# State space loop with MLP items closed by GpSimd: how far GpSimd's inflows may run ahead of VectorE's scans

## The reference

```python
u, z = silu(conv(x @ W_in[:, :512])), x @ W_in[:, 512:]
delta = softplus(low_rank(u) @ W_dt + b_dt)
h = h * exp(delta_t * A) + delta_t * B_t * u_t      # over the 512 rows t, 16 states n
y = sum_n(h[:, n] * C_t[n]) + u * D
out = (y * silu(z)) @ W_out
mlp = (silu(x @ gate) * (x @ up)) @ down            # gate, up, down made from spline points
```

## Time and profile before

| | us |
|---|---|
| median of 3 runs (1773.16 to 1775.78) | 1775.08 |
| the profiled execution | 1770.57 |
| its span in the profile | 1768.8 |
| first loop, first scan to last product | 752.1 to 897.2 |
| second loop | 930.3 to 1073.5 |

### The profile page before, as it was taken

One profiled execution on the slowest core, in us unless ns is written; L12 is line 12 of the kernel. 1 busy time (PEld: TensorE's weight loads), 2 busy tenths in 40 slices (PEclk: granted clock), 3 DMA queues, 4 the chain that ended last, 5 costly groups with the idle time before them and its releaser, 6 DMA issues. The chain is left out here.

```text
span 1768.8 us, 26131 instructions
## 1 busy us (share of the span) xinstructions
PE 1557.7 (88%) x8448; PEld 1216.3 (69%) x8448; DVE 1230.9 (70%) x2538; ACT 938.2 (53%) x2019; POOL 732.4 (41%) x662
## 2 busy tenths in 40 slices
PE   6998958979999898888888887889999897999899
PEld 4777658967777788544533454667888686888787
DVE  5888847657787678799979995346666534666643
ACT  5555445855665556574447443235665444656543
POOL 5999833324221333187728774112212241122222
PEclk9999989989999999999999999999999998999999
DMA  3221122111112121000000000011111111111211
GB/s 124 75 73 60 36 95 86 61 52 34 48 39 87 60 87 58 27 1 1 1 27 1 1 1 6 6 33 39 47 47 63 40 68 58 49 41 39 72 54 48
DMA packets 29565, 81.47 MB, mean 46 GB/s; under 512 B 6036, under 2 KB 10904, under 8 KB 27304
## 3 DMA queue, kind: packets, MB, share of 16 engines
q1 hardware_dynamic: 28296, 74.05, 12.9%
q0 software_dynamic: 1184, 6.37, 1.1%
HBM read 79.36 MB, written 1.05 MB: 45 GB/s over the span
## 5 line engine op out<-in xcount | busy, mean ns | idle before, releaser
L880 POOL TENSOR_TENSOR head_low<-head,head_high 128x512 fp32r<-128x512 f32 x64 | 81.8, 1279 | 457.1 <-ACT head_high L870 456.4
L1779 POOL TENSOR_TENSOR experts_low<-experts,experts_high 128x1536 fp32r<-128x1536 f32 (+1 forms) x64 | 144.8, 2266 | 281.2 <-ACT experts_high L1725 160.6
L2303 POOL TENSOR_TENSOR rings<-du,Bs 128x512 f32<-128x512 f32 x126 | 195.1, 1558 | 111.5 <-DVE du L2192 68.5
L1232 ACT ACTIVATE probs<-banks,neg_max 128x512 f32<-128x512 f32 (+3 forms) x256 | 131.6, 527 | 151.2 <-DVE neg_max L1142 151.2
L2023 PE MATMUL banks<-rings,ident 128*128 128x512 f32 x256 | 138.6, 632 | 30.7 <-DVE rings L2256 30.3
L2217 DVE TENSOR_TENSOR_SCAN state<-banks,rings 128x512 f32<-128x512 f32 x128 | 154.9, 1211 | 2.6 <-POOL rings L2303 1.9
L218 PE MATMUL banks<-experts_high,xnT_high 128*128 128x384 f32 (+1 forms) x384 | 139.5, 363 | 7.8 <-POOL experts_low L1779 7.8
L1476 DVE SCALAR_TENSOR_TENSOR hidden<-banks,weight,act_out 128x96 f32<-128x96 f32 (+1 forms) x192 | 62.6, 368 | 115.0 <-ACT act_out L1444 114.5
L1444 ACT ACTIVATE act_out<-banks 128x256 f32<-128x256 f32 (+2 forms) x112 | 47.5, 424 | 173.1 <-PE banks L218 172.8
L218 PE MATMUL banks<-experts_high,xnT_low 128*128 128x384 f32 (+1 forms) x384 | 137.4, 358 | 0.0
L218 PE MATMUL banks<-experts_low,xnT_high 128*128 128x384 f32 (+1 forms) x384 | 137.3, 358 | 0.0
(11 more groups left out here) (288 smaller groups left out, 4723.5 us busy)
## 6 DMA issues: line engine op xcount, KB each, us to landing
head<-in_heads SPq DMA_DIRECT2D x64, 384.0 KB, 3.1
experts<-in_experts SPq DMA_DIRECT2D x16, 1152.0 KB, 5.2
experts<-in_experts SPq DMA_DIRECT2D x16, 768.0 KB, 4.2
values<-in_values SPq DMA_DIRECT2D x32, 256.0 KB, 3.1
coef<-in_spline_coef POOLq DMA_DIRECT2D x8, 768.0 KB, 4.6
idx<-in_lut_idx SPq DMA_DIRECT2D x16, 134.0 KB, 2.1
x<-in_x SPq DMA_DIRECT2D x2, 512.0 KB, 4.6
w_in<-in_w_in SPq DMA_DIRECT2D x1, 1024.0 KB, 5.7
```

Source lines behind the costliest of these rows:

```text
L1232: last = nc.scalar.activation(prob_tile(i), score_tile(i), ACT.Exp, bias=neg_max[:, i:i + 1], scale=QK_SCALE, accum_out=row_sum[:, i:i + 1])
L1779: nc.gpsimd.tensor_tensor(parts[gpar][1][:, columns], raw[gpar][:, columns], parts[gpar][0][:, columns].bitcast(FP32), ALU.subtract)\
L2303: nc.gpsimd.tensor_tensor(inflow[:, step % INFLOWS], du[:, c], Bs[:, n], ALU.mult)\
```

## The change

GpSimd's wait before inflow s is for scan s-2 instead of scan s-4. The number of slots stays four. Nothing else differs.

```diff
--- before.py
+++ after.py
@@ -1843,7 +1843,7 @@
     y_taken, gated_y, joined = m.sig("y_taken"), m.sig("gated_y"), m.sig("joined")
     multiplied, bent, hidden_ready = m.sig("gate_up_done"), m.sig("gated"), m.sig("hidden_ready")
     dve_chain = m.sig("dve_chain")
-    DECAYS, INFLOWS, PRODUCTS = 2, 4, 3
+    DECAYS, INFLOWS, PRODUCTS, AHEAD = 2, 4, 3, 2
     STEPS = KC * NS
 
 
@@ -2299,7 +2299,7 @@
                 pool.wait_ge(du_ready.sem, du_ready.at(2))
             if step >= INFLOWS:
 
-                pool.wait_ge(scanned.sem, scanned.at(step + 1 - INFLOWS + DECAYS))
+                pool.wait_ge(scanned.sem, scanned.at(step + 1 - AHEAD + DECAYS))
             nc.gpsimd.tensor_tensor(inflow[:, step % INFLOWS], du[:, c], Bs[:, n], ALU.mult)\
               .then_inc(inflow_ready.sem, 1)
             if step in FINISH_AT:
```

## The result

| | before | after |
|---|---|---|
| median | 1774.05 (6 runs, 1770.8 to 1775.8) | 1787.39 (6 runs, 1782.0 to 1790.9) |
| profiled execution / span | 1770.57 / 1768.8 | 1787.02 / 1785.2 |
| both loops together, first scan to last product | 145.0 + 143.2 = 288.3 | 151.8 + 149.4 = 301.2 |

The ratio of the runs is 1.0075 (95% interval 1.0062 to 1.0088): slower by 13.3 us. The loops of the two profiled executions are 12.9 us apart, so the loss lies in them; the other 3.5 us between the two spans lie outside, 2.8 of them ahead of the first loop, where nothing changed.

What follows compares the result with a forecast made beforehand. VectorE's chain of scan and product was taken as the bound; the terms 0.5+0.2+3.2+0.8+0.1+2.5 = +7.3 us on the median of 1775.1 gave 1782, with 8 in 10 from 1769 to 1795.

Steps and rivals of the forecast that it cites:

- rival 3: Same mechanism, with the waits nearer 0.9 us and early conflicts gone: 1773 to 1778 us, chance 0.26.
- the signs named: Profile after: held-up products 12 to 15 us; first loop's tanh wait some 9, GpSimd's scan wait 25 or more.
- A quiet step costs nothing: In an undisturbed loop step the inflow is 0.5 us early for its scan: cost 0.
- The wait binds at nearly all steps: GpSimd really waits for scan s-2 before inflow s at nearly all of the 120 steps.
- The handoff: From inflow to scan, unseen when tight: at least 0; if 0.6 us, 0.1 at each of some 100 steps, +10.
- A new wait of 1.43 where items are three apart: GpSimd's later finish delays ScalarE's tanh, so VectorE's next gate waits 1.43 us where MLP items are three steps apart.
- item 2 with its 1.15 on top: Second MLP item: 1.43 us plus 1.15, as step 16's delta product precedes finish 1 in GpSimd's queue; 2.6.
- Where items are four apart a product loses 0.64: The finish comes in time for tanh but pushes the next inflow into the product: 0.64 us.
- Norm and residual sum: Middle steps: two small VectorE instructions meet GpSimd work, +1.4 and +0.6 us; first-loop residual sum: product 43 -1.07, 44 +0.4.
- Items 5 and 9: MLP items: 5, in the early steps, costs 0.64 us; 9, in the middle, is covered by the norm.
- rival 1: GpSimd recovers no lateness between items, scans wait for inflows, 24 us at most: 1790 to 1800 us, chance 0.18.
- rival 2: GpSimd always behind the product, which never waits; 25.4 us go, 5 and 12 x 0.7 come: 1763 us, chance 0.17.

Runs made afterwards that it cites:

- the changed kernel with z moved: Changed kernel with TensorE's z projection of block 3 in step 37 instead of 38: 1779.53 us, ratio 1.0035.
- the late finish with lead four: Kernel before (lead four) with the finishes of items 6 to 15 two inflows later, behind g+7 instead of g+5: 1781.72 us, ratio 1.0042.
- rows copied ahead: Changed kernel with ScalarE's B or C row copy ahead of the half gate in four steps (items 1, 2, 4, 6): 1784.90 us, ratio 1.0064.
- the faster kernel: Changed kernel with the finish behind inflow g+3 instead of g+5 and z of block 3 projected in step 37 instead of 38: 1768.12 us, ratio 0.9959.
- short lead with early finish: Changed kernel (lead two) with each finish behind inflow g+3 instead of g+5: 1775.49 us, ratio 1.0002.

## Why the prediction was right, and what it missed

The forecast was slower, 1782; measured 1787.4, inside the range, with +13.3 us where the sum had +7.3. Balance within 0.2% (rival 3) is excluded by the interval, which starts at 1.0062. Of the signs named, products held up came to 10.5 us (12 to 15 forecast), the wait for tanh in the first loop to 13.2 (some 9), GpSimd's wait for scans to 31.3 (25 or more), and ScalarE's half gate waited 20.4 us in 11 waits. Scan starts set side by side give each part. Scan 32 starts 66.96 us behind scan 0 before and 69.31 after in the first loop, 66.65 and 68.79 in the second; scan 47 stands 109.67 and 113.44, and 108.77 and 112.45.

| part | forecast | measured |
|---|---|---|
| to scan 32 | +0.5, +0.8 | +2.35, +2.14 |
| scan 32 to 47 | +0.2, +0.1 | +1.42, +1.54 |
| scan 47 to the end | +3.2, +2.5 | +3.03, +2.45 |

- *A quiet step costs nothing*: right. *The wait binds at nearly all steps* was too much: of the 60 inflows from step 4 to 63, 40 in the first loop and 43 in the second start within 0.2 us of their scan's end; at the others GpSimd still had a finish or other work ahead of them. To step 9 the scans stay 1.72 apart (0.18 lie between the two kernels at most), inflows take 1.56 to 1.64 and end 0.5 us before their scan. The handoff, bounded at +10, costs nothing; the one scan that waited for an inflow (0.8, scan 21, as forecast with item 3) began 0.03 behind its end.
- *A new wait of 1.43 where items are three apart*: right, 1.36 or 1.37, but for 1.66 at item 1 of the first loop; item 2 with its 1.15 on top was 2.59, forecast 2.6.
- *Where items are four apart a product loses 0.64*: right at items 3, 13 and 15 (products of 1.30 or 1.31); item 11 of the first loop took 0.64 too, where I had 0.33. Together with the waits at 12 and 14 this gives the last part.
- *Norm and residual sum*: right. In the first loop the two small instructions took 1.00 and 0.65, and product 44 took 2.61, forecast 0.66 + 1.9; rows of before are the earlier trace rows.

```profile
857.26 1.00 DVE L226 TENSOR_TENSOR rs<-rs 128x8 f32<-128x8 f32 x1
858.29 0.65 DVE L227 TENSOR_TENSOR rs<-rs 128x8 f32<-128x8 f32 x1
...
864.07 2.61 DVE L2256 TENSOR_TENSOR rings<-state,Cs 128x512 f32<-128x512 f32 x1
```

- *Items 5 and 9* are the terms mis-sized. "Item 5: 0.64" was 1.79: product 26 waited 1.27 for the row and then lost 0.52. "Items 9 and 10 are covered by the norm" was wrong for item 9: its gate stands on TensorE's z projection, and came 1.70 later in both loops (1.06 more wait, 0.64 of product 40). Together 2 x (1.15 + 1.70) = 5.7 us, about what the sum lacks (12.9 less 7.3 = 5.6). The step that failed: I followed who waits for tanh on VectorE and left TensorE at its old cost, though I had to name what is queued behind the waiting half gate on ScalarE, the row copies, and who waits for them.
- *Both terms hang on TensorE's half clock*, by the loops in which it stayed away. Without the fall near step 23 (the second loop of the changed kernel with z moved, where the idle time ahead of it was shorter too) product 26 took 1.30 with no wait: the 0.64 forecast. Without the fall near step 40 (both loops of the late finish with lead four, the first loop with rows copied ahead) gate 9 started 3.59 us behind its scan, as before. Without the two 7.2 of the 12.9 are left, with small misses that cancel: 1.2 and 1.0 up to scan 32, -0.3 and -0.2 from there to scan 47, where the sum had 0.5, 0.8, 0.2 and 0.1.
- *GpSimd no longer fits* (rival 1): excluded, since released inflows take 1.63, only scan 21 waited for one, and the faster kernel keeps the lead of two. By this the full block of the Trainium skill (SBUF — State Buffer, Who interferes with whom) isn't met by this pair: an inflow behind a product loses 0.37 of the product's 0.50.
- *Faster* (rival 2) has its mechanism: 15 us less of held-up products. It needed the finish to come in time, as it does in the kernel that beats both.

Both halves of the test show that the waits at gates 1, 2, 4, 6, 12 and 14 are the late finish (late finish with long lead: they come at 12 and 14; short lead with early finish: they go, but for the 0.72 of before at gate 12 of the second loop). The 1.70 us at gate 9 of each loop are not: they stay with the early finish, do not come with the late finish and the long lead, and stand only where the clock fell. That the falls follow from idle time is argued from the order of events alone. What makes the same idle stretch of 3.1 us drop the clock in nearly every loop with the lead of two and in none with the lead of four stays open.

## What to carry to other kernels

When a queue is tied more closely to another engine, look at what stands behind the waiting instruction, and move that with it: here the same wait cost 13 us with the finish at g+5 and, with z moved, gained 8 with the finish at g+3. An engine whose work holds up the bounding one can be released by the instruction ahead of the one it must not collide with: here that took the time lost on products from 26.7 us to 16.7 in the faster kernel. Follow each new wait through every queue to TensorE, and count there the clock as well as the wait.

## What the runs showed of the hardware

- Product and inflow (128x512, float32, inputs in SBUF): a product begun first loses nothing, and the inflow takes 1.63 us instead of 1.26 where 0.50 of the product were left, 1.76 where 0.63 were left. A product begun second ends 0.55 us behind the inflow, with 0.16 to 0.97 us of the inflow left (27 pairs before, 0.546 to 0.551).
- TensorE's clock fell inside a stage in which it is busy 83% of the time (126.75 of 152.0 us, first loop after), behind idle stretches of 2.2 and 3.1 us: with the clock at half until 850.8, the z projection's four matrix products took 3.1 us from start to last end (848.30 to 851.44), before 1.9 (843.41 to 845.29), in TensorE's timeline after and before:

```profile
848.30 1.91 PE L1931 MATMUL banks<-xmT,w_in 128*128 128x512 f32 x2
850.01 1.43 PE L1931 MATMUL banks<-xn,w_in 128*128 128x512 f32 x2
```

```profile
843.41 1.02 PE L1931 MATMUL banks<-xmT,w_in 128*128 128x512 f32 x2
844.27 1.02 PE L1931 MATMUL banks<-xn,w_in 128*128 128x512 f32 x2
```

The Trainium skill (TensorE: Matmul & The Clock Gate, HAM oscillation — how this bites in real kernels) describes such falls behind waits between bursts of matrix products; the granted clock of 0.50 at 847.4 to 850.8 agrees.
